# Target rows of a graph-attention kernel: the first chunk formed straight from PSUM

## What is computed

```python
Wh = h @ W
e = (Wh @ a_src)[:, None] + (Wh @ a_dst)[None, :]
e = jnp.where(e > 0, e, ALPHA * e)             # ALPHA = 0.2
scores = jnp.where(adj > 0, e, NEG_BIG)
attention = jax.nn.softmax(scores, axis=1)
h_prime = attention @ Wh
```

## Time and profile before

| | before |
|---|---|
| median of three runs | 651.01 us |
| the profiled execution, its own time | 648.58 us |
| its span (first to last instruction) | 646.5 us |
| mean granted clock of TensorE, as a share of full speed | 0.952 |
| VectorE idle before L1116, waiting for ScalarE's L372 | 7.7 us in 3 places |

### The profile page before, as it was taken

One profiled execution on the slowest core, in us unless ns is written; L12 is line 12 of the kernel. 1 busy time (PEld: TensorE's weight loads), 2 busy tenths in 40 slices (PEclk: granted clock), 3 DMA queues, 4 the chain that ended last, 5 costly groups with the idle time before them and its releaser, 6 DMA issues.

```text
span 646.5 us, 7470 instructions
## 1 busy us (share of the span) xinstructions
PE 569.7 (88%) x3130; PEld 195.1 (30%) x3169; DVE 361.8 (56%) x490; ACT 278.8 (43%) x297; POOL 31.9 (5%) x28
## 2 busy tenths in 40 slices
PE   5534999999999999999989998999769899999997
PEld 3301223333223344222233222245332222333332
DVE  2985766546766536766646766534989966000010
ACT  1573455434555432555532555335848666100000
POOL 0500000201000101000000000022000000000000
PEclk9556999999999999999998999999979999899999
DMA  8990000000000000000000000000000000000000
GB/s 358 368 399 11 1 0 2 1 0 1 2 1 0 1 0 3 0 1 2 0 1 1 1 0 2 0 2 1 0 1 0 2 1 0 1 1 0 1 0 33
DMA packets 3041, 19.33 MB, mean 30 GB/s; under 512 B 320, under 2 KB 320, under 8 KB 960
## 3 DMA queue, kind: packets, MB, share of 16 engines
q1 hardware_dynamic: 2864, 17.83, 6.8%
q10 hardware_dynamic: 144, 1.03, 0.5%
HBM read 18.33 MB, written 0.52 MB: 29 GB/s over the span
## 4 chain that ended last, share of the span: by engine, by line
PE 65%; DVE 21%; issue 5%; ACT 4%; DMA 2%; POOL 1%; POOLq 0%; DVEq 0%; ACTq 0%
PE PROD L653 14%; PE X L854 9%; PE S L665 9%; PE X L645 8%; PE PROD L854 7%; DVE X L1129 6%; DVE aB L1335 5%; ACT big L382 2%; DVE nadj L1238 2%; PE M L631 2%; PE X L545 2%; DMA big<-in_adjT 2%; PE S L869 2%; DVE big L1116 1%; POOL rr L319 1%
## 5 line engine op out<-in xcount | busy, mean ns | idle before, releaser
L382 ACT ACTIVATE big<-X,v 128x1024 f32<-128x1024 f32 x128 | 137.3, 1112 | 139.8 <-PE X L645 139.4
L1129 DVE SCALAR_TENSOR_TENSOR X<-wB,v,aB 128x1024 f32<-128x1024 f32 x128 | 161.5, 1289 | 59.3 <-ACT big L382 57.9
L653 PE MATMUL PROD<-big,Wh 128*64 128x512 f32 x512 | 125.9, 609 | 0.5 <-ACT big L382 0.2
L645 PE MATMUL X<-nadj,bigI 128*128 128x512 bf16 x233 | 67.3, 386 | 23.4 <-DVE X L1129 19.7
L665 PE MATMUL S<-big,onesf 128*32 128x512 f32 x512 | 68.2, 605 | 0.6 <-ACT big L382 0.6
L653 PEld LDWEIGHTS PROD<-big,Wh 128*64 128x64 f32 x512 | 30.2, 136 | 81.1 <-ACT big L382 49.8
L645 PEld LDWEIGHTS X<-nadj,bigI 128*128 128x128 bf16 x256 | 15.8, 97 | 95.8 <-DVE X L1129 72.6
L319 POOL TENSOR_TENSOR rr<-var,mhalf 128x8 f32<-128x8 f32 x8 | 17.3, 2161 | 371.5 <-DVE var L995 371.5
L854 PE MATMUL PROD<-nadj,Wh 128*64 128x512 f32 x128 | 30.3, 602 | 2.9 <-ACT nadj L473 2.9
L631 PE MATMUL M<-big,level 128*32 128x512 fp8e4 x256 | 19.8, 439 | 14.0 <-ACT big L421 11.7
L854 PE MATMUL PROD<-big,Wh 128*64 128x512 f32 x128 | 31.3, 606 | 0.7 <-ACT big L473 0.5
(11 more groups left out here) (266 smaller groups left out, 574.9 us busy)
## 6 DMA issues: line engine op xcount, KB each, us to landing
big<-in_adjT SPq DMA_DIRECT2D x13, 1024.0 KB, 7.9
aB<-in_adjT SPq DMA_DIRECT2D x3, 1024.0 KB, 8.8
cst<-in_cst ACTq DMA_DIRECT2D x1, 1008.5 KB, 5.6
x<-in_xT SPq DMA_DIRECT2D x1, 512.0 KB, 6.2
out<-x SPq DMA_DIRECT2D x2, 256.0 KB, 2.0
```

What stands on the lines that cost most here:

```text
L382: act.activation(prob[:, t % U, :], X[t % 2][:], ACT.Exp, bias=v2[l % 2][:, k:k + 1]).then_inc(p_ready, 1)
L645: last = pe.matmul(X[t % 2][:, hh * BANK:(hh + 1) * BANK], bigI[:], nadj[:, k, half_cols(c, hh)], start=False, stop=True, skip_group_check ...
L653: last = pe.matmul(PROD[c][feat(hh), :], Wh[l % 2][:, k, :], prob[:, t % U, hh * BANK:(hh + 1) * BANK], start=k == 0, stop=k == NB - 1)
L1129: dve.scalar_tensor_tensor(X[t % 2][:], wB[:, cols(c)], v8[l % 2][:, k:k + 1], aB[:, cols(c)], ALU.max, ALU.add).then_inc(x_written, 1)
```

## The change

For chunk 0, ScalarE no longer copies the code sums out of PSUM. VectorE's `target_first` and `target_second` read X[0] themselves, with per-partition scales (`nvs2` = 0.2 times the scale, and `nvs`). The offset that ScalarE used to add is put into the sum in PSUM beforehand: TensorE's `code_origin` writes it into both banks of X[0] by a product of one row (`origin`, one value, broadcast to 128 columns) with a row of 512 ones, and the products of L638 for q = 0 and 1 now add to it. Chunk 1 keeps ScalarE's copies.

`code_origin` stands before `top_levels` for l = 0, 1, 2, and in the middle of it (before block 8) for l = 3. The dummies of L634 go to X[1] in place of X[0]; of the seven dummies at the end of the layers 0 and 1 one stays. POOL writes two more constants at the start, VectorE makes `nvs2` and, for l = 3, `origin` (behind a wait for `nvb`).

```diff
@@ gpsimd, at the start
             pool.memset(mhalf[:], -0.5).then_inc(consts, 1)
+            pool.memset(ones_row[:], 1.0).then_inc(consts, 1)
+            pool.memset(origin[:], -(LOW * WIN + LEAN + SPAN / 2)).then_inc(consts, 1)
@@ scalar
             def shift_rows(l):
                 act.wait_ge(nv_param, 1 + l // FIX)
-                for q in range(4):
+                for q in (2, 3):
@@ tensor
+            def code_origin(l):
+                pe.wait_ge(nv_param, 1 + l // FIX)
+                for q in range(2):
+                    pe.matmul(X[0][:, q * BANK:(q + 1) * BANK], origin[0:1, l:l + 1].broadcast_to([1, P]), ones_row[:],
+                              start=True, stop=False)
@@ top_levels
+                    if l == 3 and jb == CB:
+                        code_origin(l)
...
-                repeat(X[0], 4)
+                repeat(X[1], 4)
                 pe.wait_ge(code_ready, l + 1)
                 for q in range(4):
                     rows = slice(WIN * q, WIN * (q + 1))
                     pe.matmul(X[q // 2][:, (q % 2) * BANK:(q % 2 + 1) * BANK], c16[rows, :], code[rows, :],
-                              start=True, stop=True).then_inc(nv_psum, 1)
+                              start=q >= 2, stop=True).then_inc(nv_psum, 1)
@@ the loop over layers
                 if l == 3:
                     repeat(X[0], 9)
+                else:
+                    code_origin(l)
                 top_levels(l)
...
-                pe.wait_ge(nv_ready, 4 * (l + 1))
+                pe.wait_ge(nv_ready, 2 * (l + 1))
...
-                    repeat(X[0], 3 if l == 2 else 7)
+                    repeat(X[0], 3 if l == 2 else 1)
@@ vector, value_range (l = 3)
                 dve.tensor_scalar(nvs[:, 3:4], rng[:, 2:3], -1.0, None, ALU.mult)
-                dve.tensor_scalar(nvb[:, 3:4], rng[:, 2:3], float(LOW * WIN + LEAN), rng[:, 1:2], ALU.mult,
-                                  ALU.add).then_inc(nv_param, 1)
+                dve.tensor_scalar(nvs2[:, 3:4], rng[:, 2:3], -SLOPE, None, ALU.mult)
+                link(dve.tensor_scalar(nvb[:, 3:4], rng[:, 2:3], float(LOW * WIN + LEAN), rng[:, 1:2], ALU.mult,
+                                       ALU.add))
+                dve.tensor_scalar(origin[:, 3:4], nvb[:, 3:4], rng[:, 3:4], -1.0, ALU.mult,
+                                  ALU.mult).then_inc(nv_param, 1)
@@ vector, target_first and target_second
+                if c == 0:
+                    dve.wait_ge(nv_psum, 4 * l + hh + 1)
+                    link(dve.scalar_tensor_tensor(tbuf[:, hh * BANK:(hh + 1) * BANK], X[0][:, b], nvs2[:, l:l + 1],
+                                                  wB[:, b], ALU.mult, ALU.subtract))
...
+                if c == 0:
+                    link(dve.scalar_tensor_tensor(aB[:, b], X[0][:, b], nvs[:, l:l + 1],
+                                                  tbuf[:, hh * BANK:(hh + 1) * BANK], ALU.mult, ALU.min))
+                    return
                 link(dve.tensor_tensor(aB[:, b], aB[:, b], tbuf[:, hh * BANK:(hh + 1) * BANK], ALU.min))
@@ exponents
                 elif k == 1:
-                    dve.wait_ge(nv_ready, 4 * (l + 1))
+                    dve.wait_ge(nv_ready, 2 * (l + 1))
```

More of the change, by code:

```diff
@@ L131, in program @@
         nvb = sb("nvb", [P, GAT])
+        nvs2 = sb("nvs2", [P, GAT])
+        origin = sb("origin", [P, GAT])
+        ones_row = sb("ones_row", [1, BANK])
         vz = sb("vz", [P, NB])
@@ L257, in program @@
         block = ctx.enter_context(nc.Block())
-        N_C = 7
+        N_C = 9
         def kept(c, k):
@@ L1102, in value_bounds @@
                 dve.tensor_scalar(nvs[:, 0:FIX], step[:], -1.0, None, ALU.mult)
+                dve.tensor_scalar(nvs2[:, 0:FIX], step[:], -SLOPE, None, ALU.mult)
                 signal(dve.scalar_tensor_tensor(nvb[:, 0:FIX], step[:], float(LOW * WIN + LEAN), bound[:], ALU.mult,
@@ L1113, in target_first @@
                 b = half_cols(c, hh)
-                dve.wait_ge(nv_ready, 4 * l + 2 * c + hh + 1)
                 dve.wait_ge(wB_ready, 2 * (2 * l + c) + hh + 1)
-                link(dve.scalar_tensor_tensor(tbuf[:, hh * BANK:(hh + 1) * BANK], aB[:, b], SLOPE, wB[:, b], ALU.mult,
-                                              ALU.subtract))
+                if c == 0:
+                    dve.wait_ge(nv_psum, 4 * l + hh + 1)
+                    link(dve.scalar_tensor_tensor(tbuf[:, hh * BANK:(hh + 1) * BANK], X[0][:, b], nvs2[:, l:l + 1],
+                                                  wB[:, b], ALU.mult, ALU.subtract))
+                else:
+                    dve.wait_ge(nv_ready, 2 * l + hh + 1)
+                    link(dve.scalar_tensor_tensor(tbuf[:, hh * BANK:(hh + 1) * BANK], aB[:, b], SLOPE, wB[:, b],
+                                                  ALU.mult, ALU.subtract))
             def target_second(l, c, hh):
                 b = half_cols(c, hh)
+                if c == 0:
+                    link(dve.scalar_tensor_tensor(aB[:, b], X[0][:, b], nvs[:, l:l + 1],
+                                                  tbuf[:, hh * BANK:(hh + 1) * BANK], ALU.mult, ALU.min))
+                    return
                 link(dve.tensor_tensor(aB[:, b], aB[:, b], tbuf[:, hh * BANK:(hh + 1) * BANK], ALU.min))
```

## The result

The changed kernel took 655.06 us (median of 8 executions, 651.49 to 657.63), the kernel before, beside it, 650.50 (648.31 to 651.77). The ratio is 1.0076 with a 95% interval of 1.0056 to 1.0097: slower, by 4.6 us between the medians (4.9 by the ratio) where 1.3 had been forecast. In a second comparison it was 1.0100 (1.0079 to 1.0121). The profiled execution is one of the shortest: 651.49 us, span 649.7 against 646.5.

What follows compares the result with a forecast made beforehand. It took a chain of waits in a serial stretch once per layer as bounding; layers 0 to 3 gave -0.53, -0.27, +0.50 and +1.58, total +1.28 us on 651.01: 652.3 us, +0.2%, range 649.3 to 655.3, chance 0.50.

Steps and rivals of the forecast that it cites:

- Head start: Layers 0, 1 and 3: VectorE starts right after TensorE's L638, without ScalarE's copy, 0.77 to 0.78 us earlier; nothing in layer 2.
- pointers: VectorE's four operations, every layer: per-partition scales read through a pointer cost 62 ns each, 0.25 us a layer.
- the further 0.26 us a layer: VectorE's four operations: extra PSUM cost by the skill's cycle table, making the sum 1.0 us worse; not taken, the trace disagreed.
- Layer 3: 1.8 and 0.3: Layer 3's path: one-row products with weight change amid the 64 products, 1.8 us; VectorE's small operations before L1052, 0.3 us.
- Layers 1 and 2: 0.25 late: Before the 64 products: new products replacing six dummies end after the levels are there, 0.25 us late in each (0 to 0.4).
- Layer 2's pointers: Layer 2: pointer scales lose 0.25 us with no head start to offset them.
- the falling clock: Rival, 64 products of layers 1 and 2: clock falls behind one-row products, 1.7 us each, 655.7 us; chance 0.17.
- The rule cited there: Against the clock's fall in layers 1 and 2: TensorE needs only no idle gaps between bursts, so the sum stands at 652.3.
- The pair loop didn't swallow the head start: Rival: the loop behind, bound by other waits, absorbs the 0.52 us, 653.9 us; chance 0.15, shared with a missing head start.
- A clock that rises sooner in layer 0: Rival, layer 0's masks: full clock one stretch sooner saves 1.7 us, 650.6 us; chance 0.18, shared with cheaper one-row products.
- layer 3's products run beside others: Layer 3: only then would the new products cost less than 1.8 us; held against it, they need all the array's columns.
- The mapping from the profile to the median: Whole kernel: the sum, +1.28 us, is a difference, holds for profiled and median executions alike, and is added to 651.01.

Runs made afterwards that it cites:

- one-row dummies: Kernel before with six of the seven dummies ending layers 0 and 1 given one row in place of 128: 651.77 us, 1.0041 of before.
- 128-row version: Changed kernel with the offset's product given 128 rows of ones times 1/128 in place of one row: 653.09 us, 1.0035; again 652.33 us, 1.0038 of before.

## Why the prediction was wrong

*The sum of the work* was right in its mechanism and its parts. Head start and pointers together: 0.53, 0.52 and 0.52 were forecast for the layers 0, 1 and 3, and 0.57, 0.55 and 0.55 measured. The pointer form takes 751 ns for the 750 taken, and PSUM costs nothing more; so the further 0.26 us a layer, worked out from the table of the Trainium skill ("VectorE: DVE Perf Modes"), isn't there in the changed kernel either. Layer 3: 1.8 and 0.3 were forecast, 2.02 and 0.31 measured. Layers 1 and 2: 0.25 late was forecast, 0.46 and 0.50 measured. This term was mis-sized: the new product starts 0.32 us behind the dummy, as costed (0.21 and 0.1), but the 64 products start 1.91 behind it, not 1.71. Layer 2's pointers show no loss: -0.05 for +0.25, since the 0.98 us that one L1121 took beside POOL's operation isn't there in after, where all four take 0.75. Total +1.57 us for +1.28.

*The step that failed* is the weighing of the falling clock: in the sum it stood at nothing. The prediction had it as a rival, with its place (the 64 products of the layers 1 and 2), its price (1.7 us each) and its time (655.7 us). Measured were 1.65 and 1.68 us, and 655.06 us. But it gave it 0.17, and half to the forecast. The reason given against it was that "the new products fill the time as fully". That is what the one-row dummies refute: TensorE was busy for 3.30 of 3.30 us and the clock fell to 0.55 behind them, 1.68 and 1.69 us in the two layers. That 655.06 lies so near 655.7 is in part luck, since executions differ in the falls and in the start.

The rule cited there, from the Trainium skill ("TensorE: Matmul & The Clock Gate", its table on why it matters for kernels), asks for no idle gaps between bursts. The runs don't bear it out as a sufficient condition: no gap, and the clock fell. A row in the prediction's hands pointed there but couldn't decide: in layer 3 the clock fell behind 3 us with three-row products and transposes, in which TensorE was also idle for 1.25 us.

*The pair loop didn't swallow the head start.* Layer 1's loop is 75.27 us in after and 75.28 in before.

*A clock that rises sooner in layer 0* didn't come (granted 0.90 from 66 to 68 us in after, 0.91 in before), nor did layer 3's products run beside others: 5.83 us for 5.75 forecast.

*The mapping from the profile to the median* was unsound. I added the sum to the median as if the clock's stretches fell alike in both kernels. They don't: work +1.57 and two falls of 1.65 and 1.68 make +4.9 us if both occur; by the ratios 4.9 and 6.5 us were measured in two comparisons of the changed kernel. The agreement of the first with the sum is no proof, since its profiled execution has neither fall. What makes the second 1.6 us larger isn't settled; the late start (3.3 us in its trace) is the nearest thing, in a share of executions that isn't known. The loop of layer 0 (76.44 us for 75.73) and the end (211.76 for 210.35) vary from one execution to the next in the kernel before too.

Also open: why the 128-row version loses 2.4 us where its work is +1.57 - 0.39 = +1.2. Its interval (1.0017 to 1.0059) takes in 1.2 us, so there may be nothing to explain; and one of its two traces has the late start (34.82 us for 32.27), which would be of the size.

## What to carry to other kernels

A dummy or cheap product that keeps TensorE busy isn't a substitute for another of the same length: count the rows, and keep the full-row ones ahead of a dense stretch that bounds. Before a serial stretch is shortened, cost what is put into its waiting time to the end of that wait: here it became the last to arrive, by 0.46 us; and put a constant into PSUM by a full-row bf16 product if the value allows it. When single executions differ by more than the sum, compare segments between two or more traces and not spans, and begin at the start of the span: a segment ahead of the change can differ by more than the change is worth.

## What was not expected of the hardware

Behind six products of 1 row by 512 columns, 0.21 us apart, the clock fell to 0.55 in the next 3.5 us, though TensorE was busy all the time; behind six of 128 rows it stayed at 1.00. The segments cost 1.68 and 1.69 us more.

The fp32 product of one row occupies TensorE as long as one of 128 (587 ns a record for 592), but it stands in the way a little longer: levels to code is 4.27 us with one row and 4.08 with 128. With one row the product starts 0.32 us behind the dummy and the 64 products 1.91 behind the product; with 128 rows it is 0.23 and 1.81. The first part shows in the weights: with 128 rows the first load at 148.47, beside the dummy's; with one row they load at 147.15, 0.32 us behind it:

```profile
148.47 0.42 PEld L629 LDWEIGHTS X<-ones_row,origin 128*128 128x128 f32 x2
```

```profile
147.15 0.29 PEld L629 LDWEIGHTS X<-ones_row,origin 1*128 1x128 f32 x2 [0.23 <-issue]
```

The operations of VectorE and POOL that run side by side in layer 2 are both faster where VectorE reads PSUM: POOL's `mix_terms` took 0.62 us in after and 1.11 before, VectorE's second operation 0.75 for 0.98, with a pointer scalar more. It is so in all thirteen traces, 0.62 us in the five with the new form in layer 2 and 1.11 or 1.12 in the eight without. The form of VectorE's operation changed together with the place of its input, so the two aren't told apart.
